# Folding a layer normalisation into centred weights and a row scale, in a graph-attention and expert kernel

## The chip, the cores and the metric

The kernel runs on one core of a Trainium2 chip. The metric is device time in microseconds (us) of one execution; shown are three runs of the kernel before and one profiled execution. The engines are TensorE (PE, with its weight loads as PEld), VectorE (DVE), ScalarE (ACT), GpSimd (POOL) and SyncE (SP), which here only issues transfers.

## The reference, cut to what matters

x is 128 graphs of 128 nodes with 256 features, adj one 128x128 matrix per graph. A graph attention comes first, then eight gated experts with three matrix products each.

```python
def _layernorm(x, axis=-1, eps=1e-5):
    m = jnp.mean(x, axis=axis, keepdims=True)
    v = jnp.var(x, axis=axis, keepdims=True)
    return (x - m) / jnp.sqrt(v + eps)
...
    Wh = jnp.einsum('bnd,df->bnf', h, W)          # h = _layernorm(x)
    s1 = Wh @ a1
    s2 = Wh @ a2
    e = s1[:, :, None] + s2[:, None, :]
    e = jnp.where(e > 0, e, ALPHA * e)
    e = e + jnp.log(adj + EPS)
    alpha_w = jax.nn.softmax(e, axis=-1)
    h_prime = jnp.einsum('bij,bjf->bif', alpha_w, Wh)
...
    x = x + _L0_gnn_ref(_layernorm(x, axis=-1), adj, L0_gnn_W, L0_gnn_a)
    x = x + _L0_ffn_ref(_layernorm(x, axis=-1), ...)
```

The change is in the first `_layernorm` and its product with `W` alone.

## The kernel before

The program has two blocks, one behind the other. The first is the attention (graph block), the second the experts (expert block). The engines meet at the border between them.

The graph block takes the graphs in 32 groups of four (`GB`), g = 0 to 31. Each engine has its own function `step(g, layer)` and runs it for every g in a row (`over_groups`), so the order of the work on an engine is the order in which `step` is written, and semaphores tie the engines together. A step works at several groups at once, by their age. Of the step that is numbered g:

- PE: transposes the attention weights of group g-2 (`ps_pT`, L741), projects group g (`ps_wide` <- `gw`, `xnT`, L730), makes the output of g-2 (`ps_th` <- `wh`, `pT`, L759, two halves of two graphs), spreads the column term s2 of g (`ps_s`, L769), transposes the normalised rows of g+1 (`ps_th` <- `ident`, `xn`, L778).
- ACT: copies `pT` (L511), takes the exponentials `e_sb` of g-1 (L518), copies the projection to `wh` (L524), normalises the rows of g+1 into `xn` (four instructions, one per graph, L501), adds s1 to give `s_sb` (L532), copies the transposed rows to `xnT` (L542), and copies the means for the second normalisation (L546).
- DVE: statistics of the rows of g+2 (`bn_stats`, L571, one per graph, and `bn_aggr`, L585), the leaky ReLU `l_sb` (L609) and the row maximum `neg_m` (L614) of g-1, a running sum `acc` for g-4 (L635, tile `resb`), `x1` of g-2 (L664, tiles `h` and `w_bc`), the weighted attention `p_sb` (L679) and its row sums (L686) of g-1, and statistics of `x1` of g-2 (L579, L590).
- POOL: from the statistics of g+2 it makes 1/sqrt(v + eps) (`rstd1`) and -mean times that (`nb1`), L400 to L407; the same for `x1` of g-3, and the other half of `acc` (L449, L453).
- SP: loads `x_sb` of g+2 (two buffers; L327), stores `x1` of g-3, loads `res` (a second copy of x, for the addition) and `adj_sb`.

On the side the steps 6 to 21 (layer 1, two per expert) prepare the first-layer weights: POOL sums pieces, in the odd step ACT rounds them (`wq_hi`, L553) and POOL then subtracts (`wq_lo`, L471). The steps 22 to 29 (layer 2) do so for the second layer (L557, L476).

Three orderings matter. The copy to `wh` of g waits for the output products of g-2 in the same step, since they read the same of the two `wh` buffers. The transposes of g+1 write the PSUM tile `ps_th` that the output products wrote, so they wait until DVE has made `x1`. SP issues the load of `x_sb` of g+2 when ACT has made `xn` of g, since it goes into the same buffer.

Ahead of step 0 PE transposes `gw` (the weights) and makes the two columns W a1 and W a2, which become columns 256 and 257 of `gw`; a projection is so 258 columns wide.

Of the kernel before, what the change touches and what calls it, by code (L numbers as in the profile page):

```python
# [38 lines left out]
def adj_ffn(nc, x, adj, gnn_w, gnn_a, wr, br, w1, b1, g1, be1, m1, v1, w2, b2, g2, be2, m2, v2, wo, bo, out):  # L39
# [17 lines left out]
    with ExitStack() as ctx:  # L57
# [127 lines left out]
        with ExitStack() as sa:  # L185
# [19 lines left out]
            minus_one = sba("minus_one", [P, GB])  # L205
            neg_mean1 = sba("neg_mean1", [P, GB])
            nb1 = [sba(f"nb1_{i}", [P, GB]) for i in range(2)]
            rstd1 = [sba(f"rstd1_{i}", [P, GB]) for i in range(2)]
            xn = sba("xn", [P, GB, D])
# [45 lines left out]
            nb1_done = sem("nb1_done", sa)  # L255
            xn_done = sem("xn_done", sa)
# [42 lines left out]
            def over_groups(eng, step):  # L299

                for i in range(-2, 2 * K0):
# [81 lines left out]
            def _(pool):  # L383
# [4 lines left out]
                nc.gpsimd.memset(minus_one[:, :], -1.0)  # L388
# [39 lines left out]
                def step(g, layer):  # L428
                    nxt = ago(g, -2)
                    if exists(nxt):  # L430
                        rstd_1(nxt)
# [14 lines left out]
                    if exists(t) and not is_step(t, G - 2) and not is_step(t, G - 1):  # L446
# [7 lines left out]
                                                ALU.add).then_inc(acc_high_done, 1)  # L454
                    if layer == 1 and g[1] == 0:
# [30 lines left out]
            def _(act):  # L486
# [8 lines left out]
                def normalise(g):  # L495

                    p = g[1]
                    act.wait_ge(nb1_done, num(g) + 1)
                    wait(act, xnT_ready, num(g))
                    for b4 in range(GB):  # L500
                        last = nc.scalar.activation(xn[:, b4, :], x_sb[p][:, b4, :], ACT.Identity,  # L501
                                                    bias=nb1[p][:, b4:b4 + 1], scale=rstd1[p][:, b4:b4 + 1])
                    last.then_inc(xn_done, 1)

                def step(g, layer):
# [20 lines left out]
                    if exists(nxt):  # L526
                        normalise(nxt)
# [37 lines left out]
            def _(dve):  # L565
# [26 lines left out]

                def step(g, layer):
                    p = g[1]
                    a = ago(g, 1)
                    r = a[1]
                    nxt = ago(g, -2)

                    def stats_part(b4):

                        if exists(nxt):
                            stats_1(nxt, b4)

                    if exists(a):

                        stats_part(0)
# [5 lines left out]
                        stats_part(1)  # L612
# [3 lines left out]
                        stats_part(2)  # L616
                        stats_part(3)
                    else:
                        for b4 in range(GB):
                            stats_part(b4)  # L620
# [5 lines left out]
                    b = ago(g, 2)  # L626
                    q = b[1]
                    t = ago(g, 3)
                    h = ago(g, 4)
                    if exists(h) and not is_step(h, G - 2) and not is_step(h, G - 1):  # L630
                        dve.wait_ge(rstd2_done, num(h) + 1)
                        dve.wait_ge(acc_low_done, num(h) + 1)
                        dve.wait_ge(mean2_done, num(h) + 1)
                        for b4 in range(HB):
                            last = nc.vector.scalar_tensor_tensor(out=acc[:, b4, :], in0=x1[h[1]][:, b4, :],  # L635
                                                                  scalar=rstd_all[:, num(h), b4:b4 + 1],
                                                                  in1=acc[:, b4, :], op0=ALU.mult, op1=ALU.add)
                        last.then_inc(acc_low_done, 1)

                    if exists(nxt):  # L640
                        dve.wait_ge(bnst1, num(nxt) + 1)
                    elif exists(b):
                        dve.wait_ge(rowsum_done, num(b) + 1)
                        if exists(t):
                            dve.wait_ge(bnst2, num(t) + 1)
                    elif exists(t):
                        dve.wait_ge(bnst2, num(t) + 1)
                    if exists(b):
                        nc.vector.reciprocal(rinv[:, :], rowsum[:, :]).then_inc(rinv_done, 1)
                    if exists(nxt):  # L650
                        aggregate_1(nxt)
                    if exists(t):
                        aggregate_2(t)
                    if exists(b):
# [5 lines left out]
                        wait(dve, x1s_high_done, num(b) - 1)  # L660
                        for b4 in range(GB):
# [8 lines left out]
                    with_stats = exists(b) and not is_step(b, G - 1)  # L670
                    if exists(a):


                        dve.wait_ge(e_done, num(a) + 1)
                        if with_stats:
                            stats_2(b, 0)
# [5 lines left out]
                        if with_stats:  # L682
                            stats_2(b, 1)
                        dve.wait_ge(p_done, num(a) + 1)
                        wait(dve, rinv_done, num(a))
                        nc.vector.tensor_reduce(rowsum[:, :], p_sb[:, :, :], AX_X, ALU.add).then_inc(rowsum_done, 1)  # L686
                    if with_stats:
                        for b4 in range(2 if exists(a) else 0, GB):
# [20 lines left out]
            def _(pe):  # L709
                pe.wait_ge(setup_done, 1)  # L710
                pe.wait_ge(proj_loaded, 2 * 16)

# [21 lines left out]
                def step(g, layer):  # L734
# [37 lines left out]
                    if exists(nxt):  # L772
                        pe.wait_ge(xn_done, num(nxt) + 1)
# [508 lines left out]
```

## Time and profile before

| | |
|---|---|
| runs | 2540.9, 2535.84, 2536.35 us, median 2536.35 |
| profiled execution | 2537.31 us; span of its instructions 2535.5 us |
| PE busy | 2412.7 us, 95% of the span |
| DVE, ACT, POOL busy | 1717.1 (68%), 1638.9 (65%), 459.4 us (18%) |
| HBM | 46 GB/s over the span |

The span is the time from the first to the last instruction of the program. Busy times overlap between engines, so the shares say which engine is full and not which one waits. The graph block is the first 390 us, some 15% of the span.

### The profile page before, as it was taken

Reading aid. Unit: us, or ns where it says so; the run is one execution under the profiler, and the core shown is the slowest. Engines: PE = TensorE matmul, PEld = TensorE weight load, DVE = VectorE, ACT = ScalarE, POOL = GpSimd, SP = SyncE. Lnnn points to the kernel's source line nnn. Section 1 sums busy time; section 2 is a strip of 40 time slices with the busy share of each in tenths; the row PEclk is TensorE's granted clock in tenths of the full one; section 3 lists DMA queues with packets and bytes.
Section 4 is the critical chain, followed back from the end, with each engine's and each line's share of the span. In section 5 each row is a group of like instructions: output and inputs, shape, how many; then the busy total and the mean of one; then the engine's idle time right before and its main releaser. Section 6 shows DMA issues by size and latency. Waiting matters only on the chain.

```text
span 2535.5 us, 45093 instructions
## 1 busy us (share of the span) xinstructions
PE 2412.7 (95%) x16304; PEld 2218.3 (87%) x16304; DVE 1717.1 (68%) x2444; ACT 1638.9 (65%) x2497; POOL 459.4 (18%) x487
## 2 busy tenths in 40 slices
PE   6777776999999999999999999999999999999999
PEld 5666665999999999999999999999999999999998
DVE  4777775666666666666666666666666666666665
ACT  4666654666666666666666666666666666666665
POOL 3566553111011111111111111111100111011110
PEclk9999997999999999999999999999999999999999
DMA  3555552000000000000000000000000000000000
GB/s 125 172 186 173 179 165 67 26 20 22 25 17 17 25 25 25 25 25 25 25 25 25 25 25 25 25 25 25 25 25 25 25 24 17 25 17 19 21 17 26
DMA packets 91178, 116.16 MB, mean 46 GB/s; under 512 B 4700, under 2 KB 78856, under 8 KB 91144
## 3 DMA queue, kind: packets, MB, share of 16 engines
q1 hardware_dynamic: 91144, 115.73, 13.9%
q8 instruction: 19, 0.31, 0.1%
q14 instruction: 15, 0.12, 0.0%
HBM read 82.16 MB, written 33.55 MB: 46 GB/s over the span
## 4 chain that ended last, share of the span: by engine, by line
PE 83%; DVE 1%; ACT 0%; issue 0%; ACTq 0%; DVEq 0%
PE ps_y L1182 29%; PE ps_wide L171 28%; PE ps_wide L1164 25%; PE ps_t L132 1%; DVE h_lo L1069 0%; DVE h L1076 0%; PE ps_y L1230 0%; DVE z L1062 0%; DVE x1t L124 0%; ACT h_hi L971 0%; DVE feat_sum L1102 0%; ACT v L976 0%; DVE resb L179 0%; DVE z L1052 0%; DVE h_lo L1084 0%
## 5 line engine op out<-in xcount | busy, mean ns | idle before, releaser
L976 ACT ACTIVATE v<-ps_wide,bn_cols 128x256 f32<-128x256 f32 x768 | 434.3, 566 | 399.3 <-PE ps_wide L1164 269.9
L984 ACT ACTIVATE h<-ps_wide,bn_cols 128x512 f32<-128x512 f32 x512 | 399.0, 779 | 327.5 <-PE ps_wide L171 327.5
L1182 PE MATMUL ps_y<-wo_lo,h_hi 128*128 128x256 f32 x2048 | 579.1, 283 | 0.0
L1182 PE MATMUL ps_y<-wo_hi,h_hi 128*128 128x256 f32 x2048 | 577.4, 282 | 1.6 <-DVE h_lo L1084 1.6
L1182 PE MATMUL ps_y<-wo_hi,h_lo 128*128 128x256 f32 x2048 | 578.6, 283 | 0.0
L1164 PE MATMUL ps_wide<-xq_hi,wq_hi 128*128 128x256 f32 x1792 | 506.2, 282 | 14.9 <-PEq L185 9.2
L1164 PE MATMUL ps_wide<-xq_lo,wq_hi 128*128 128x256 f32 x1792 | 509.7, 284 | 0.0
L1164 PE MATMUL ps_wide<-xq_hi,wq_lo 128*128 128x256 f32 x1792 | 507.1, 283 | 0.0
L1084 DVE TENSOR_TENSOR h_lo<-h,h_hi 128x1024 fp32r<-128x1024 f32 x256 | 318.2, 1243 | 238.9 <-ACT h_hi L990 238.9
L1062 DVE SCALAR_TENSOR_TENSOR z<-ps_wide,bn_cols,v 128x512 f32<-128x512 f32 x256 | 192.2, 751 | 318.0 <-PE ps_wide L1164 318.0
L171 PE MATMUL ps_wide<-h_hi,w_hi 128*128 128x512 f32 x1024 | 404.3, 395 | 2.1 <-DVE h_lo L1069 2.1
L171 PE MATMUL ps_wide<-h_lo,w_hi 128*128 128x512 f32 x1024 | 405.6, 396 | 0.0
L171 PE MATMUL ps_wide<-h_hi,w_lo 128*128 128x512 f32 x1024 | 405.5, 396 | 0.0
L1069 DVE SCALAR_TENSOR_TENSOR h_lo<-z,h_hi 128x1024 fp32r<-128x1024 f32 x256 | 316.3, 1236 | 120.7 <-ACT h_hi L971 120.7
L1182 PEld LDWEIGHTS ps_y<-wo_hi,h_hi 128*128 128x128 f32 x2048 | 386.7, 189 | 1.9 <-DVE h_lo L1084 1.8
L1182 PEld LDWEIGHTS ps_y<-wo_hi,h_lo 128*128 128x128 f32 x2048 | 387.5, 189 | 0.0
L1182 PEld LDWEIGHTS ps_y<-wo_lo,h_hi 128*128 128x128 f32 x2048 | 386.6, 189 | 0.0
L1164 PEld LDWEIGHTS ps_wide<-xq_hi,wq_hi 128*128 128x128 f32 x1792 | 341.1, 190 | 27.6 <-issue 10.0
L954 POOL TENSOR_TENSOR resb<-resb,bias_out 128x1024 f32<-128x1024 f32 x32 | 85.2, 2663 | 1535.3 <-DMA resb<-x_scratch 1535.3
L1164 PEld LDWEIGHTS ps_wide<-xq_hi,wq_lo 128*128 128x128 f32 x1792 | 338.4, 189 | 10.0
L1164 PEld LDWEIGHTS ps_wide<-xq_lo,wq_hi 128*128 128x128 f32 x1792 | 339.9, 190 | 0.0
L1076 DVE TENSOR_TENSOR h<-h,w_bc 128x1024 f32<-128x1024 f32 x256 | 312.9, 1222 | 7.5 <-ACT w_bc L1018 4.6
(131 smaller groups left out, 3118.9 us busy)
## 6 DMA issues: line engine op xcount, KB each, us to landing
x_sb<-in_x SPq DMA_DIRECT2D x32, 512.0 KB, 3.9
res<-in_x SPq DMA_DIRECT2D x32, 512.0 KB, 5.8
x1t<-x_scratch SPq DMA_DIRECT2D x32, 512.0 KB, 3.3
resb<-x_scratch SPq DMA_DIRECT2D x32, 512.0 KB, 3.3
out<-resb SPq DMA_DIRECT2D x32, 512.0 KB, 3.0
adj_sb<-in_adj SPq DMA_DIRECT2D x32, 256.0 KB, 6.0
x_scratch<-h SPq DMA_DIRECT2D x16, 512.0 KB, 4.7
x_scratch<-w_bc SPq DMA_DIRECT2D x16, 512.0 KB, 4.5
```

What stands on the lines that cost most here:

```text
L132: last = nc.tensor.transpose(ps_x[:, c, b4 * N:(b4 + 1) * N], x1t[:, b4, c * P:(c + 1) * P], ident[:, :])
L171: mm = nc.tensor.matmul(acc_ps, w[:, i, c, cols], s[:, c, :], start=start and n == 0, stop=stop and n == len(terms) - 1)
L954: nc.gpsimd.tensor_tensor(resb[:, :, :], resb[:, :, :], bias_out[:, None, :].to_broadcast([P, GB, D]), ALU.add).then_inc(resb_done, 1)
L976: nc.scalar.activation(v[:, slot, :], ps_l1[:, 0, 0:H], ACT.Identity, bias=bn_cols[:, 1, cols], scale=bn_cols[:, 0, cols]).then_inc(done, 1)
L984: nc.scalar.activation(h2[:, m, :], ps_l2[:, m, :], ACT.Relu, bias=bn_cols[:, 3, cols], scale=bn_cols[:, 2, cols]).then_inc(r2_done, 1)
L1062: nc.vector.scalar_tensor_tensor(out=z[:, 0, :], in0=ps_l1[:, 1, :], scalar=bn_cols[:, 0, C * e:C * e + 1], in1=v[:, 0:2, :].rearrange("p ...
L1069: nc.vector.scalar_tensor_tensor(out=h1_lo[:, :, :], in0=z[:, :, :], scalar=0.0, in1=h1_hi[:, :, :].bitcast(F32), op0=ALU.max, op1=ALU.sub ...
L1076: nc.vector.tensor_tensor(h2w[:, :, :].rearrange("p c (b n) -> p (c b) n", n=N), h2[:, :, :].rearrange("p c (b n) -> p (c b) n", n=N), w_b ...
L1084: nc.vector.tensor_tensor(h2_lo[p][:, :, :], h2w[:, :, :], h2_hi[p][:, :, :].bitcast(F32), ALU.subtract).then_inc(lo2_done, 1)
L1164: mm = nc.tensor.matmul(out_ps, w[:, e, q, :], x[:, q, :], start=start and n == 0, stop=stop and n == len(terms) - 1, skip_group_check=True)
L1182: mm = nc.tensor.matmul(ps_y[:, b4, :], h[:, c, cols], w[:, e, c, :], start=(e == 0 and k == 0 and b4 % per_bank == 0), stop=(e == E - 1 a ...
```

## The change

The normalised rows (x - mean) r, with r = 1/sqrt(v + eps) of the row, times W, are the same as r times x (W - column means of W). The change uses that:

- Setup: POOL fills `mean_w` with 1/256. Two PE products of 256 columns (L704 of the changed kernel) put the column means of `gw` in all rows of a PSUM tile, and DVE subtracts them from `gw` (L582, 128x512) before `gw` is transposed. `neg_mean1`, `nb1`, `minus_one` and `xn` go.
- ACT no longer makes `xn` (four instructions of 128x256 with a pointer for bias and one for scale). PE transposes `x_sb` itself. The copy to `wh`, one instruction of 128x1032, becomes four of 128x258, each with `rstd1` as a pointer for scale, and also waits for `rstd1`.
- DVE takes the statistics of g+1 in place of g+2, behind `x1` of g-2 and around `p_sb`, and no longer at the start of its step; `bn_aggr` stands behind the row sums. The two `acc` additions stand on both sides of `neg_m`.
- POOL makes `rstd1` of g+1 at the end of its step, behind the work for the second normalisation: two instructions in place of four.
- SP issues the load of g+2 when PE has transposed `x_sb` of g and DVE has taken its statistics.
- The loop begins at -1, no longer at -2.

```diff
@@ load
-                    wait(sp, xn_done, num(g) - 1)
+                    wait(sp, xnT_ready, num(g) - 1)
+                    wait(sp, bnst1, num(g) - 1)
@@ rstd_1 on POOL
-                    wait(pool, nb1_done, num(g))
-                    nc.gpsimd.tensor_tensor(ve1[:, :], mv1[p][:, :, 1], eps_cols[:, :], ALU.add)
-                    nc.gpsimd.tensor_tensor(neg_mean1[:, :], mv1[p][:, :, 0], minus_one[:, :],
-                                            ALU.mult).then_inc(ve1_done, 1)
+                    wait(pool, rstd1_done, num(g))
+                    nc.gpsimd.tensor_tensor(ve1[:, :], mv1[p][:, :, 1], eps_cols[:, :],
+                                            ALU.add).then_inc(ve1_done, 1)
                     pool.wait_ge(ve1_done, num(g) + 1)
+                    wait(pool, wh_copied, num(g) - 1)
                     nc.gpsimd.tensor_tensor(rstd1[p][:, :], ve1[:, :], minus_half[:, 0:GB],
                                             ALU.pow).then_inc(rstd1_done, 1)
-                    pool.wait_ge(rstd1_done, num(g) + 1)
-                    nc.gpsimd.tensor_tensor(nb1[p][:, :], neg_mean1[:, :], rstd1[p][:, :],
-                                            ALU.mult).then_inc(nb1_done, 1)
@@ ACT
                     if exists(g):
                         act.wait_ge(wh_ready, num(g) + 1)
+                        act.wait_ge(rstd1_done, num(g) + 1)
                         wait(act, h_ready, num(g) - 1)
-                        nc.scalar.activation(wh[p][:, :, :], ps_wide[:, :, 0:D + 2], ACT.Copy).then_inc(wh_copied, 1)
+                        for b4 in range(GB):
+                            last = nc.scalar.activation(wh[p][:, b4, :], ps_wide[:, b4, 0:D + 2], ACT.Copy,
+                                                        scale=rstd1[p][:, b4:b4 + 1])
+                        last.then_inc(wh_copied, 1)
                     nxt = ago(g, -1)
-                    if exists(nxt):
-                        normalise(nxt)
@@ DVE, setup
+                dve.wait_ge(col_mean_ready, 1)
+                nc.vector.tensor_tensor(gw[:, :, 0:D], gw[:, :, 0:D], ps_wide[:, 0:1, 0:D].to_broadcast([P, C, D]),
+                                        ALU.subtract).then_inc(gw_centred, 1)
@@ PE
+                for c in range(C):
+                    last = nc.tensor.matmul(ps_wide[:, 0, 0:D], mean_w[:, :], gw[:, c, 0:D], start=(c == 0),
+                                            stop=(c == C - 1))
+                last.then_inc(col_mean_ready, 1)
+                pe.wait_ge(gw_centred, 1)
...
-                        pe.wait_ge(xn_done, num(nxt) + 1)
+                        pe.wait_ge(x_loaded[nxt[1]], 16 * (nxt[0] + 1))
...
                                 last = nc.tensor.transpose(ps_xT[:, c, b4 * N:(b4 + 1) * N],
-                                                           xn[:, b4, c * P:(c + 1) * P], ident[:, :])
+                                                           x_sb[nxt[1]][:, b4, c * P:(c + 1) * P], ident[:, :])
```

On ACT a whole step of the graph block, as the program lists it, is this before (tile, source, shape, number):

```order
L511 ACTIVATE pT<-ps_pT 128x512
L518 ACTIVATE e_sb<-l_sb,neg_m 128x128 x4
L524 ACTIVATE wh<-ps_wide 128x1032
L501 ACTIVATE xn<-x_sb,nb_0,rstd_0 128x256 x4
L532 ACTIVATE s_sb<-ps_s,wh 128x128 x4
L542 ACTIVATE xnT<-ps_th 128x1024
L546 ACTIVATE mean_all<-mv_0 128x4
```

and this in the changed kernel, at the same place:

```order
L497 ACTIVATE pT<-ps_pT 128x512
L504 ACTIVATE e_sb<-l_sb,neg_m 128x128 x4
L512 ACTIVATE wh<-ps_wide,rstd_0 128x258 x4
L520 ACTIVATE s_sb<-ps_s,wh 128x128 x4
L530 ACTIVATE xnT<-ps_th 128x1024
L534 ACTIVATE mean_all<-mv_1 128x4
```

The row of `xn` is gone, and the copy to `wh` has four parts and reads `rstd`.

On DVE a step ran in this order (from the start of the step, step 5 of the graph block, to `p_sb`):

```order
L571 BN_STATS st<-x_sb 128x6
L609 SCALAR_TENSOR_TENSOR l_sb<-s_sb 128x512
L571 BN_STATS st<-x_sb 128x6
L614 TENSOR_REDUCE neg_m<-l_sb 128x4
L571 BN_STATS st<-x_sb 128x6 x2
L635 SCALAR_TENSOR_TENSOR resb<-w_bc,rstd_all,resb 128x256 x2
L649 RECIPROCAL rinv<-rowsum 128x4
L585 BN_AGGR mv_1<-st 128x2 x4
L590 BN_AGGR mv_0<-st 128x2 x4
L664 SCALAR_TENSOR_TENSOR w_bc<-ps_th,rinv,res 128x256 x4
L579 BN_STATS st<-w_bc 128x6
L679 SCALAR_TENSOR_TENSOR p_sb<-adj_sb,e_sb 128x512
```

and in the changed kernel the same step runs so:

```order
L617 SCALAR_TENSOR_TENSOR l_sb<-s_sb 128x512
L621 RECIPROCAL rinv<-rowsum 128x4
L578 BN_AGGR mv_0<-st 128x2 x4
L604 SCALAR_TENSOR_TENSOR resb<-w_bc,rstd_all,resb 128x256
L627 TENSOR_REDUCE neg_m<-l_sb 128x4
L604 SCALAR_TENSOR_TENSOR resb<-w_bc,rstd_all,resb 128x256
L647 SCALAR_TENSOR_TENSOR w_bc<-ps_th,rinv,res 128x256 x4
L559 BN_STATS st<-x_sb 128x6 x2
L661 SCALAR_TENSOR_TENSOR p_sb<-adj_sb,e_sb 128x512
L559 BN_STATS st<-x_sb 128x6 x2
L567 BN_STATS st<-w_bc 128x6
L674 TENSOR_REDUCE rowsum<-p_sb 128x4
```

The statistics of x have moved from ahead of `l_sb` to behind `x1` (tile `w_bc`), and nothing of `x_sb` stands between the step's start and `x1` any more. PE's order is the same in both, but for the two products at the start; only what the transposes read and wait for differs.

## Rows read from the trace of the kernel before

**Rows 1.** Page: busy share in 40 equal slices, and granted PE clock, in tenths.

```profile
PE   6777776999999999999999999999999999999999
PEclk9999997999999999999999999999999999999999
```

**Rows 2.** Timeline, 204 to 218 us, all engines: start us, length us.

```profile
204.34 0.39 SPq L327 DMA_DIRECT2D x_sb<-in_x  x1
...
206.43 3.75 PE L730 MATMUL ps_wide<-gw,xnT 128*128 128x258 f32 x16 [0.68 <-ACT xnT L542]
...
208.39 0.43 DVE L571 BATCH_NORM_STATS2 st<-x_sb 128x6 f32<-128x256 f32 x1 [2.17 <-DMA x_sb<-in_x]
...
210.02 1.89 PE L759 MATMUL ps_th<-wh,pT 128*128 128x256 f32 x8
...
210.36 1.28 ACT L518 ACTIVATE e_sb<-l_sb,neg_m 128x128 f32<-128x128 f32 x4 [3.41 <-DVE neg_m L614]
...
212.01 1.03 ACT L524 ACTIVATE wh<-ps_wide 128x1032 f32<-128x1032 f32 x1 [0.36 <-PE ps_th L759]
...
212.93 2.06 ACT L501 ACTIVATE xn<-x_sb,nb,rstd 128x256 f32<-128x256 f32 x4
...
213.09 1.16 PE L769 MATMUL ps_s<-ident,wh 128*128 128x128 f32 x8 [1.18 <-ACT wh L524]
...
214.90 1.11 ACT L532 ACTIVATE s_sb<-ps_s,wh 128x128 f32<-128x128 f32 x4
215.05 1.09 PE L778 MATMUL ps_th<-ident,xn 128*128 128x128 f32 x8 [0.80 <-ACT xn L501]
...
216.18 1.02 ACT L542 ACTIVATE xnT<-ps_th 128x1024 f32<-128x1024 f32 x1 [0.16 <-PE ps_th L778]
...
217.25 3.75 PE L730 MATMUL ps_wide<-gw,xnT 128*128 128x258 f32 x16 [0.68 <-ACT xnT L542]
```

**Rows 3.** Groups, 100 to 400 us, shapes apart: busy us, mean ns.

```profile
L501 ACT ACTIVATE xn<-x_sb,nb,rstd 128x256 f32<-128x256 f32 x96 | 49.5, 588 | 0.0
...
L571 DVE BATCH_NORM_STATS2 st<-x_sb 128x6 f32<-128x256 f32 x88 | 34.8, 416 | 54.9 <-DMA x_sb<-in_x 54.9
...
L532 ACT ACTIVATE s_sb<-ps_s,wh 128x128 f32<-128x128 f32 x100 | 27.9, 358 | 1.2 <-PE ps_s L769 1.2
...
L524 ACT ACTIVATE wh<-ps_wide 128x1032 f32<-128x1032 f32 x25 | 25.6, 1024 | 16.4 <-PE ps_th L759 16.4
...
L511 ACT ACTIVATE pT<-ps_pT 128x512 f32<-128x512 f32 x26 | 15.3, 589 | 2.6 <-PE ps_pT L741 2.6
```

**Rows 4.** Timeline of PE, projections and one transpose of 30 steps.

```profile
38.97 3.79 PE L730 MATMUL ps_wide<-gw,xnT 128*128 128x258 f32 x16 [0.26 <-ACT xnT L542]
...
69.29 1.52 PE L778 MATMUL ps_th<-ident,xn 128*128 128x128 f32 x8 [0.80 <-ACT xn L501]
71.93 4.37 PE L730 MATMUL ps_wide<-gw,xnT 128*128 128x258 f32 x16 [0.26 <-ACT xnT L542]
...
361.52 3.75 PE L730 MATMUL ps_wide<-gw,xnT 128*128 128x258 f32 x16 [0.68 <-ACT xnT L542]
```

**Rows 5.** Busy time and granted clock (after POOL's entry) by stretch.

```profile
70.00:71.00 1.00, 1.00 (x6) 1.00 (x5) 0.69 (x3) 0.40 (x2) 0.92 (x2) 0.50 0.81 72
...
200.00:250.00 50.00, 37.58 (x200) 30.94 (x199) 40.29 (x129) 34.19 (x80) 31.73 (x49) 0.97 0.51 163
```

**Rows 6.** Timeline, 196 us: POOL and DVE side by side.

```profile
196.34 2.08 POOL L471 TENSOR_TENSOR wq_lo<-w_stage,wq_hi 128x896 f32 x1 [1.11 <-ACT wq_hi L553]
...
196.74 2.23 DVE L609 SCALAR_TENSOR_TENSOR l_sb<-s_sb 128x512 f32<-128x512 f32 x1
```

**Rows 7.** Timeline of the start, PE and DVE.

```profile
15.95 6.71 PE L730 MATMUL ps_wide<-gw,xnT 128*128 128x258 f32 x16 [1.40 <-ACT xnT L542]
...
27.95 3.75 PE L730 MATMUL ps_wide<-gw,xnT 128*128 128x258 f32 x16 [1.11 <-ACT xnT L542]
...
29.70 0.43 DVE L571 BATCH_NORM_STATS2 st<-x_sb 128x6 f32<-128x256 f32 x1 [12.80 <-DMA x_sb<-in_x]
```

More of the change, by code:

```diff
@@ L204, in adj_ffn @@
             ve1 = sba("ve1", [P, GB])
-            minus_one = sba("minus_one", [P, GB])
-            neg_mean1 = sba("neg_mean1", [P, GB])
-            nb1 = [sba(f"nb1_{i}", [P, GB]) for i in range(2)]
+            mean_w = sba("mean_w", [P, P])
             rstd1 = [sba(f"rstd1_{i}", [P, GB]) for i in range(2)]
-            xn = sba("xn", [P, GB, D])
             xnT = sba("xnT", [P, C, T])
@@ L299, in over_groups @@
             def over_groups(eng, step):
-                for i in range(-2, 2 * K0):
+                for i in range(-1, 2 * K0):
                     step((i // 2, i % 2), 0)
@@ L493, in _ @@
                                      ACT.Copy).then_inc(va_copied, 1)
[L495 to L503, printed above, removed]
                 def step(g, layer):
@@ L591, in aggregate_2, with add_part @@
                     last.then_inc(stats2_done, 1)
+                dve.wait_ge(col_mean_ready, 1)
+                nc.vector.tensor_tensor(gw[:, :, 0:D], gw[:, :, 0:D], ps_wide[:, 0:1, 0:D].to_broadcast([P, C, D]),
+                                        ALU.subtract).then_inc(gw_centred, 1)
                 def step(g, layer):
-                    p = g[1]
                     a = ago(g, 1)
+                    b = ago(g, 2)
+                    t = ago(g, 3)
+                    h = ago(g, 4)
                     r = a[1]
[L597 to L602, printed above, removed]
+                    q = b[1]
+                    nxt = ago(g, -1)
+                    with_acc = exists(h) and not is_step(h, G - 2) and not is_step(h, G - 1)
+                    with_stats = exists(b) and not is_step(b, G - 1)
+                    def add_part(b4):
+                        if not with_acc:
+                            return
+                        if b4 == 0:
+                            dve.wait_ge(rstd2_done, num(h) + 1)
+                            dve.wait_ge(acc_low_done, num(h) + 1)
+                            dve.wait_ge(mean2_done, num(h) + 1)
+                        part = nc.vector.scalar_tensor_tensor(out=acc[:, b4, :], in0=x1[h[1]][:, b4, :],
+                                                              scalar=rstd_all[:, num(h), b4:b4 + 1],
+                                                              in1=acc[:, b4, :], op0=ALU.mult, op1=ALU.add)
+                        if b4 == HB - 1:
+                            part.then_inc(acc_low_done, 1)
+                    if exists(b):
+                        dve.wait_ge(rowsum_done, num(b) + 1)
+                    if exists(t):
+                        dve.wait_ge(bnst2, num(t) + 1)
                     if exists(a):
-                        stats_part(0)
                         dve.wait_ge(s_done, num(a) + 1)
@@ L615, in step @@
                                                 negate=True).then_inc(neg_m_done, 1)
[L616 to L620, printed above, removed]
+                    add_part(1)
                     if is_step(g, G - 1):
@@ L625, in step @@
                         tile_normalise(dve, 0, range(HB, GB))
[L626 to L653, printed above, removed]
                     if exists(b):
@@ L669, in step @@
                         last.then_inc(x1_done, 1)
-                    with_stats = exists(b) and not is_step(b, G - 1)
+                    if exists(nxt):
+                        wait(dve, rstd1_done, num(nxt) - 1)
+                        stats_1(nxt, 0)
+                        stats_1(nxt, 1)
                     if exists(a):
                         dve.wait_ge(e_done, num(a) + 1)
-                        if with_stats:
-                            stats_2(b, 0)
                         dve.wait_ge(adj_loaded[r], 16 * (a[0] + 1))
@@ L686, in step @@
                         nc.vector.tensor_reduce(rowsum[:, :], p_sb[:, :, :], AX_X, ALU.add).then_inc(rowsum_done, 1)
+                    if exists(nxt):
+                        aggregate_1(nxt)
                     if with_stats:
-                        for b4 in range(2 if exists(a) else 0, GB):
+                        for b4 in range(1, GB):
                             stats_2(b, b4)
```

33 lines of the change are left out of this document (24 added, 9 removed).

## The prediction

> **What bounds the kernel now.** I read the page first. PE is busy 9 tenths or more from the seventh slice on, with the full clock, and 5 to 7 tenths before [rows 1]. The reader is to see two programs: an expert block in which PE is full, which this change doesn't touch, and a graph block of some 370 us in which PE is not full and something goes round in a ring. All that can be won or lost lies there (and at its two ends).
>
> Then the timeline of one step. Follow PE from one projection to the next, 206.43 to 217.25, which is 10.82 us [rows 2]. The projection and the output products end at 210.02 + 1.89 = 211.91. ACT's copy to `wh` starts 0.10 later. It takes 1.03, and the normalisation of the next rows ends at 214.99. PE waits 0.80 for that and transposes (1.09), ACT copies the result (1.02, start 216.18), and the next projection starts at 217.25 [rows 2]. Nothing in this ring has slack: it is PE, ACT, PE, ACT, PE. The column term (`ps_s`, 1.16) and `s_sb` (1.11) lie beside the normalisation and cost nothing [rows 2].
>
> A second ring is nearly as long. ACT ends `xn`, SP issues a load at 204.34, DVE waits 2.17 us for it and starts at 208.39; the leaky ReLU and the maximum stand behind this, and ACT waits 3.41 for the maximum before it takes the exponentials (210.36 to 211.64), which stand ahead of the copy to `wh` [rows 2]. Here that left 0.36 us to spare. Over the block DVE waited 54.9 us for x [rows 3].
>
> Thirty projections stand between 38.97 and 361.52: 322.55 us, or 11.12 for each of 29 steps [rows 4]. 29 undisturbed steps would be 29 x 10.82 = 313.8. The other 8.8 us are two things. First the clock: it fell to half seven times in this stretch, each time as the transposes ran or were about to. In the fall at 69.8 the transposes took 1.52 in place of 1.09 and the projection 4.37 in place of 3.75 [rows 2, 4, 5], so 1.05 us; at 1.0 each, 7.0. Ahead of such a fall PE had waited 1.18 us, spread the column term, and waited 0.80 [rows 2]. Second, eight odd steps with `wq_lo` on POOL: `l_sb` on DVE took 2.23 us beside POOL's 2.08 [rows 6], the exponentials came late, and that leaves 1.8 us for all.
>
> **The change, part by part.** *The normalisation goes, the copy to `wh` grows.* The price of one 128x258 copy with one pointer has no row of its own. Its nearest is `s_sb`: from PSUM, one pointer, 128 columns, 358 ns [rows 3]. The slope of ACT per column is (1024 - 589) / (1032 - 512) = 0.84 ns, from two plain copies out of PSUM [rows 3]; 130 more columns are 109 ns, so 467. Four `s_sb` take 1.11 [rows 2], so the next starts 251 ns after the one before, and 107 of 358 overlap. Four copies: 467 + 3 x 360 = 1.55 us. From below: without a price for the pointer, 376 and 3 x 269, 1.18 us. From above: like `xn`, with two pointers and 256 columns, 2.06 us [rows 2]. I take 1.55, since `s_sb` has the same source and one pointer, and keep 1.18 and 2.06 for the range.
>
> The Trainium skill, page "ScalarE: Activation LUTs", section "What ACT_TABLE_LOAD costs", gives an instruction with immediates 186 ns + 0.833 per column, 93 more for each pointer, and an overlap of about 93; by that estimate the four would take 1.70, and the sum below would be some 4 us less.
>
> *The new ring.* Output products end, 0.10, copy to `wh` 1.55, 0.05, column term 1.16, 0.03, `s_sb` 1.12 less 0.11 by which the next instruction on ACT starts before its end, copy to `xnT` 1.02, 0.05, projection and output products 5.48 (206.43 to 211.91) [rows 2]. The transposes stand right behind the column term on PE and take 1.09, so they lie beside `s_sb`. Sum: 0.10 + 1.55 + 0.05 + 1.16 + 0.03 + 1.01 + 1.02 + 0.05 + 5.48 = 10.45 us, 0.37 less than now. So of the 2.06 us of ACT work that goes only 0.37 come out, because the column term and `s_sb` lose their cover: they were beside the normalisation and are now in the ring. 29 x 0.37 = 10.7 us.
>
> *The load of x.* The transposes of g now free the buffer a step ahead of its next reader, and DVE reads it a step later. From the issue (as now, 204.34) to the first statistics, right behind `x1` of the next step but one, there are more than 15 us, against 4.05 now [rows 2]. The wait goes. The projection no longer waits for the chain behind it.
>
> *DVE's step.* What it does per step is the same: 40.29 us busy of 50, 9.0 per step of 11.12 [rows 5]. In a step of 10.45 there is room. Late next would be the exponentials. `s_sb` is ready 3.9 us behind the start of the copy to `wh`; DVE is free about 5 behind it (x1, four statistics, `p_sb`, row sums, two aggregations, three more statistics); `l_sb`, the reciprocal, an aggregation, half the `acc` and the maximum take 2.3, so the exponentials end at 8.6, against 10.45. If `wq_lo` (2.08 [rows 6]) blocks one of them, 10.3 to 10.6: just covered or 0.2 late. I count the 1.8 us as won, and in eight steps 0.2 as lost (1.6).
>
> *POOL and SP.* `rstd1` is made at 4 to 6 us of a step and read at 10.45: covered. Queued behind it are only the weight pieces, which have two steps. SP's loads wait for things of the step before; behind them stand a store and two loads that have a step to spare.
>
> *The clock.* Between the output products and the transposes PE now waits 1.18 + 0.80; it will wait 1.55 + 0.15 once, and column term and transposes run on without a gap. Less idle time in sum (1.70 for 1.98) but in one piece. That could end the falls or make them more frequent. No row decides it; I take two for seven, 5.0 us won, and keep both ends (7.0 won, 8.4 lost).
>
> *The start.* Four more PE records at the half clock (6.71 / 16 = 0.42 each [rows 7]) and one DVE instruction of 512 columns, near the 0.59 of a copy of that size [rows 3], some 2.4 with the waits. The first normalisation (2.06) goes. So +0.5. The first step (15.95 to 27.95) has the same ring: -0.37. The second, 27.95 to 38.97, took 11.02 because DVE sat until 29.70 for x [rows 4, 7]; without output products its ring is 10.45 - 5.48 - 0.10 + 3.75 + 0.05 = 8.67: -2.35.
>
> *The end.* The last steps have no normalisation before either, and a longer copy to `wh`: +0.5.
>
> **Sum.** 10.7 + 1.8 - 1.6 + 5.0 - 0.5 + 0.37 + 2.35 - 0.5 = 17.6 us off the profiled execution's 2537.31, so 2519.7. That execution is 1.0 above the median of the runs (2536.35), so a run is 2519 us.
>
> **The rivals.**
> 1. *The clock falls in every second step.* 14 or 15 falls at 1.1 in place of seven at 1.0: 17.6 - 5.0 - 8.4 = 4.2 won, 2532. For it: one wait of 1.70 is longer than either of now. Against: PE's work behind it has no gap.
> 2. *Slower: the copy to `wh` costs like `xn`.* At 2.06 the ring is 10.96, and 29 x 0.14 = 4.1 are lost; from 1.92 on the ring is no shorter than now. PE's wait is then 2.2 us in one piece, and the falls of rival 1 come with it: -4.1 + 1.8 - 1.6 - 8.4 + 1.7 = -10.6, 2547; without more falls 2539. Against: `s_sb` shows what one pointer costs.
> 3. *No change: DVE ends last.* If POOL's instructions block DVE's in all steps and not only in eight, the exponentials come at 10.8 or later, the ring is as now, and only the start and a part of the clock are won: 2533 to 2538. The Trainium skill, page "GPSIMD Engine Reference", section "Specifications", says that GpSimd shares its SBUF interface with VectorE instructions that have two SBUF inputs, as `l_sb` and the `acc` additions have. The trace agrees in the one pair [rows 6]. Against: POOL's other instructions are mostly 1 us or less.
> 4. *Better: the copy is near 1.2 us.* Ring 10.1, but then the exponentials (10.2) end last: 2513.
>
> **How the numbers follow.** Chances: the forecast with few or no falls 0.55; rival 1 0.16; rival 2 0.12; rival 3 0.10; rival 4 0.07. This kernel's measurement tells 0.2%, 5 us, from no change. Faster: the forecast, rival 4 and half of rival 1, 0.70; within 5 us: the other half of rival 1 and most of rival 3, 0.17; slower 0.13. The forecast's own range is 2514 to 2526. The range for 8 in 10 goes from rival 4's side to rival 1 and the near end of rival 3: 2512 to 2537.
>
> **What would show it.** Right: DVE waits for x no more; four copies to `wh` take 1.5 to 1.6 in sum; steps of 10.4 to 10.5 from projection to projection; `xnT` starts as `s_sb` ends; the second step is near 8.7. Wrong: copies over 1.8; the exponentials ending right ahead of the copy to `wh` in steps without `wq_lo`; more stretches at a clock of 0.50 than now; or a wait of PE for `x_sb`.

## The result, and the profile after

| | before | after |
|---|---|---|
| median of the runs | 2536.19 us (4 runs) | 2515.58 us (4 runs, 2515.3 to 2516.79) |
| profiled execution, span | 2537.31, 2535.5 us | 2515.62, 2513.8 us |
| ratio after / before | | 0.9915, 95% interval 0.9898 to 0.9933 |
| third projection starts | 38.97 us | 36.08 us |
| last projection, 29 steps on | 361.52 us | 340.77 us |
| first product of the expert block | 390.19 us | 370.19 us |

The change is 20.6 us faster, where 17 were forecast and the range was 2512 to 2537. Nearly all of it, 20.0 us, lies ahead of the expert block. The other 1.7 of the 21.7 by which the spans differ lie in the expert block, which the change doesn't touch. In the profiled executions of the ten kernels of this document that block took between 2143.6 and 2146.6 us, so a difference of this size says nothing of an edit in the graph block.

Every time here is a median; one execution of `stats_first` (3429.95 us, mean granted clock 0.65) and one of the kernel before that was timed beside it (8351.13 us) are far outside the rest and left out.

The page of the changed kernel, busy share and granted clock of PE in 40 slices, is to be laid beside [rows 1]:

```profile
PE   6777769999999999999999999999999999999999
PEclk9999988999999999999999999999999999999999
```

PE gets full from the seventh slice on, one earlier than before (there it was the eighth, and not the seventh as the prediction reads it). Its timeline for one step (start us, length us; in brackets the idle time before and what ended it), to be laid beside [rows 2]:

```profile
204.23 3.76 PE L726 MATMUL ps_wide<-gw,xnT 128*128 128x258 f32 x16 [0.84 <-ACT xnT L530]
...
205.31 2.08 POOL L467 TENSOR_TENSOR wq_lo<-w_stage,wq_hi 128x896 f32 x1 [0.59 <-ACT wq_hi L541]
205.39 2.29 DVE L604 SCALAR_TENSOR_TENSOR resb<-h,rstd_all,resb 128x256 f32<-128x256 f32 x1
...
207.60 0.67 DVE L627 TENSOR_REDUCE neg_m<-l_sb 128x4 f32<-128x512 f32 x1
207.83 1.89 PE L755 MATMUL ps_th<-wh,pT 128*128 128x256 f32 x8
...
208.31 1.28 ACT L504 ACTIVATE e_sb<-l_sb,neg_m 128x128 f32<-128x128 f32 x4 [2.71 <-DVE neg_m L627]
...
209.76 1.58 ACT L512 ACTIVATE wh<-ps_wide,rstd 128x258 f32<-128x258 f32 x4 [0.17 <-PE ps_th L755]
...
211.39 1.16 PE L765 MATMUL ps_s<-ident,wh 128*128 128x128 f32 x8 [1.67 <-ACT wh L512]
...
212.38 1.04 PE L774 MATMUL ps_th<-ident,x_sb 128*128 128x128 f32 x8
...
212.58 1.14 ACT L520 ACTIVATE s_sb<-ps_s,wh 128x128 f32<-128x128 f32 x4 [1.25 <-PE ps_s L765]
...
213.60 1.04 ACT L530 ACTIVATE xnT<-ps_th 128x1024 f32<-128x1024 f32 x1
...
214.69 3.76 PE L726 MATMUL ps_wide<-gw,xnT 128*128 128x258 f32 x16 [0.84 <-ACT xnT L530]
```

Read it as the prediction's ring: output products end at 209.72, the four copies to `wh` take 1.58, the column term follows 0.05 behind them, the transposes run on behind it without a wait, and `xnT` starts as `s_sb` ends. From projection to projection it is 10.46 us. The next step, without `wq_lo`, takes 10.54, since its copy to `wh` starts 0.12 behind the output products (end 220.18) in place of 0.04:

```profile
220.30 1.58 ACT L512 ACTIVATE wh<-ps_wide,rstd 128x258 f32<-128x258 f32 x4 [1.91 <-PE ps_th L755]
```

The projections of the first steps and the last (timeline of PE), beside [rows 4, 7]:

```profile
16.57 5.81 PE L726 MATMUL ps_wide<-gw,xnT 128*128 128x258 f32 x16 [1.40 <-ACT xnT L530]
...
27.35 3.76 PE L726 MATMUL ps_wide<-gw,xnT 128*128 128x258 f32 x16 [1.27 <-ACT xnT L530]
...
36.08 3.76 PE L726 MATMUL ps_wide<-gw,xnT 128*128 128x258 f32 x16 [0.84 <-ACT xnT L530]
...
340.77 3.76 PE L726 MATMUL ps_wide<-gw,xnT 128*128 128x258 f32 x16 [0.84 <-ACT xnT L530]
```

The groups between 100 and 370 us (busy us, mean ns of one, idle before them and what ended it), beside [rows 3]. DVE waits for x no more (0.0 against 54.9):

```profile
L512 ACT ACTIVATE wh<-ps_wide,rstd 128x258 f32<-128x258 f32 x96 | 37.8, 477 | 27.2 <-PE ps_th L755 27.2
...
L559 DVE BATCH_NORM_STATS2 st<-x_sb 128x6 f32<-128x256 f32 x92 | 34.2, 412 | 0.0
```

And the windows of 100 to 360 us (busy of PE, PEld, DVE, ACT, POOL, then the granted clock), first before:

```profile
100.00:360.00 260.00, 198.39 (x1026) 163.54 (x1027) 200.25 (x626) 171.79 (x393) 162.23 (x232) 0.96 0.55 178
```

and after:

```profile
100.00:360.00 260.00, 195.28 (x1071) 164.18 (x1070) 226.54 (x670) 144.67 (x385) 163.36 (x192) 0.99 0.58 186
```

Between the first step and 355.3 us no stretch at half clock is left; before there were eight, seven of them in the 29 steps. The clock of 0.99 over the window is the stretch from 355.3 on, where PE waits at the block's end. So 29 steps gave 322.55 - 304.69 = 17.9 us, in two parts. The undisturbed ring gave 313.8 (29 x 10.82) less 304.5 (15 x 10.54 and 14 x 10.46), which is 9.3. What was lost beside it, 8.8 us before, is 0.2 now: 8.6 more. Those 8.6 are the falls of the clock and the late odd steps together.

### The profile page after: what moved, and what is told of

It is laid out like the page before. It is cut to its first block, busy times and chain, and to the rows that moved or that the text cites. A ratio compares the mean times of both kernels' runs of the same rounds, so it can differ in the third digit from the quotient of the medians.

```text
span 2513.8 us, 45142 instructions
## 1 busy us (share of the span) xinstructions
PE 2397.0 (95%) x16308; PEld 2209.6 (88%) x16308; DVE 1729.6 (69%) x2445; ACT 1596.0 (63%) x2465; POOL 453.7 (18%) x423
## 4 chain that ended last, share of the span: by engine, by line
PE 84%; DVE 1%; ACT 0%; issue 0%; ACTq 0%
PE ps_y L1178 29%; PE ps_wide L171 29%; PE ps_wide L1160 26%; PE ps_t L132 1%; DVE h_lo L1065 0%; DVE h L1072 0%; PE ps_y L1226 0%; DVE z L1058 0%; ACT v L972 0%; DVE h_lo L1080 0%; ACT h_hi L986 0%; ACT h_hi L967 0%; ACT w_bc L1014 0%; ACT h L980 0%; DVE z L1048 0%
```

## The experiments

Three questions: whether the clock's falls cost what the prediction took, and what ends them; what the copy's price does to the ring; and what the late statistics bring. Then a version that the trace suggested. Each kernel was timed against the kernel before (medians beside them 2536.8 to 2538.5 us); the steps quoted are from one projection to the next.

### Two pointers in the copy to `wh`

The changed kernel, with the four copies given a second pointer, to a column of zeros. The numbers are the same. This brings about rival 2's price.

```diff
-                            last = nc.scalar.activation(wh[p][:, b4, :], ps_wide[:, b4, 0:D + 2], ACT.Copy,
-                                                        scale=rstd1[p][:, b4:b4 + 1])
+                            last = nc.scalar.activation(wh[p][:, b4, :], ps_wide[:, b4, 0:D + 2], ACT.Identity,
+                                                        bias=zero_col[:, :], scale=rstd1[p][:, b4:b4 + 1])
```

> The changed kernel, with a second pointer (a bias column of zeros) on each of the four copies to wh. Computes the same. Theory (the step is a ring through the copies, and the clock falls where PE waits long in one piece): the four copies take about 2.05 in place of 1.58 us, the ring becomes 10.50 + 0.47 = 10.97, 14 us in 30 steps, and PE's wait of 2.2 us brings stretches at a clock of 0.50 back, 5 or more, 5 to 13 us: 2535 to 2543. Rival (the falls went for another reason, such as the transposes of raw rows): no falls, 2529 to 2530. Second rival (the copies have slack): 2516.

Measured: 2537.93 us (10 runs), 1.0002 of before, interval 0.9992 to 1.0011: the whole win is gone. The four copies take 1.94, not the 2.05 expected. The edit also turns `Copy` into `Identity`; `s_sb` is an `Identity` with one pointer, and its price gave that of a `Copy` with one pointer within 10 ns, so the second pointer is the likely cause, but no run separates the two. The timeline shows the dearer copy and PE's longer wait:

```profile
78.56 1.94 ACT L514 ACTIVATE wh<-ps_wide,zero_col,rstd 128x258 f32<-128x258 f32 x4 [3.26 <-PE ps_th L757]
...
80.55 1.16 PE L767 MATMUL ps_s<-ident,wh 128*128 128x128 f32 x8 [2.11 <-ACT wh L514]
```

Undisturbed steps are 10.81 and 10.89, 0.35 longer than after, which is 10 us in 29. The rest is the clock. It falls again in the middle of the block, at 69.8, 114.2, 158.6, 202.9 and further on, and in the first of these the transposes took 1.85 in place of 1.04. PE's wait was 2.03 or 2.11 in nearly every step, and nine of the 29 had a fall: such a wait doesn't bring one each time. The window of the first:

```profile
69.80:73.20 3.40, 3.14 (x15) 2.74 (x13) 3.18 (x16) 2.69 (x7) 1.46 (x4) 0.50 0.07 14
```

### The same, with PE kept busy in the wait

Six products of the identity with itself, into a tile that is free then, between the output products and the column term. They change no number of the kernel's.

```diff
+                    if exists(b):
+                        for b4 in range(6):
+                            nc.tensor.matmul(ps_pT[:, b4 % GB, :], ident[:, :], ident[:, :], start=True, stop=True)
                     if exists(g):
                         pe.wait_ge(wh_copied, num(g) + 1)
```

> The kernel two_pointers, and PE does six more products of ident with itself (12 records of 128 columns, about 1.5 us) into the free ps_pT in its wait between the output products and the column term; nothing reads them. Theory: ring as in two_pointers, 10.97, but no stretch at a clock of 0.50 inside the graph block: 2529 to 2531, so the difference of the two kernels is the price of the falls. Rival (the ring alone makes the time, the clock is not bound to PE's waits): the same time as two_pointers.

Measured: 2528.49 us (6 runs), 0.9969 (0.9957 to 0.9982). The steps are still 10.81 and 10.89, and after one fall in the start (33 to 37 us) the clock doesn't fall until 378 us, as the window of the steps shows:

```profile
100.00:350.00 250.00, 213.97 (x1294) 188.63 (x1294) 203.78 (x624) 145.31 (x361) 155.15 (x182) 1.00 0.58 185
```

So of the 22.4 us that the second pointer costs, 9.4 are the clock's falls and 12.9 the longer ring, with what it adds at the start and the end. With a wait of PE of 2.0 to 2.1 us there were falls, with 1.7 to 1.8 in the changed kernel there were none.

### The kernel before, with PE kept busy in its second wait

Three such products between the column term and the transposes, in the kernel before.

```diff
                         last.then_inc(s2b_ready, 1)
+                    if exists(b):
+                        for b4 in range(3):
+                            nc.tensor.matmul(ps_pT[:, b4 % GB, :], ident[:, :], ident[:, :], start=True, stop=True)
                     if exists(nxt):
                         pe.wait_ge(xn_done, num(nxt) + 1)
```

> The kernel before, and PE does three more products of ident with itself (6 records of 128 columns, about 0.75 us) into the free ps_pT in its wait of 0.80 us between the column term and the transposes; nothing reads them. Theory: the eight falls of the clock in the graph block go, the undisturbed step stays 10.82, and about 7 us are won: 2529. Rival (the falls are not bound to this wait, or the products lengthen the ring): 2536 or more, with falls.

Measured: 2529.34 us (9 runs), 0.997 (0.996 to 0.998), 7.9 us faster. The timeline of PE has its 0.80 wait filled, and from output products to transposes nothing else moved; the window behind it has the full clock:

```profile
209.85 1.16 PE L769 MATMUL ps_s<-ident,wh 128*128 128x128 f32 x8 [1.18 <-ACT wh L524]
210.84 0.83 PE L774 MATMUL ps_pT<-ident 128*128 128x128 f32 x6
211.81 1.09 PE L781 MATMUL ps_th<-ident,xn 128*128 128x128 f32 x8
```

```profile
100.00:360.00 260.00, 211.14 (x1197) 176.85 (x1198) 202.70 (x637) 174.09 (x400) 163.45 (x235) 1.00 0.56 181
```

All seven falls of the 29 steps are gone; one in the start, at 35.8, stays. The traces put less on them than the medians do: the 29 steps take 316.42 us (39.07 to 355.49) in place of 322.55, so 6.1, and the graph block is 6.0 shorter. The steps with `wq_lo` are 11.09 with the clock full, 0.27 over the 10.82 of the others. So of the 8.8 us lost beside the undisturbed ring before, 6.1 were the falls and 2.6 late steps, mostly those with `wq_lo` (the prediction had 7.0 and 1.8). All in all the falls cost 6 to 8 us.

The falls needed PE's second wait: with the 0.80 filled and the 1.18 as it was, there were none in the steps. But most steps of the kernel before had both waits and no fall. The change has one wait of 1.67 to 1.75 in their place and no gap behind it, and its trace has no fall in the steps.

### The kernel before, with the statistics of x late

Here DVE takes the statistics of x behind `x1`, as in the change, and POOL makes `rstd1` and `nb1` at its step's end; the normalisation stays on ACT.

```diff
@@ POOL: rstd_1(nxt) from the step's start to behind the acc addition
@@ DVE: ahead of l_sb, between l_sb, neg_m and acc
-                        if exists(nxt):
-                            stats_1(nxt, b4)
@@ DVE: behind x1, around p_sb
+                    if exists(nxt):
+                        stats_1(nxt, 0)
+                        stats_1(nxt, 1)
...
+                    if exists(nxt):
+                        stats_1(nxt, 2)
+                        stats_1(nxt, 3)
```

> The kernel before with only the order of DVE and POOL changed: the statistics of x of g+2 behind x1 and around p_sb, their aggregation behind the row sums, and rstd1 and nb1 at the end of POOL's step. Normalisation, transposes and copies stay. Theory: DVE waits for x no more, undisturbed step still 10.82 since that ring has no DVE in it; won are the late odd steps (1.8 us) and about 2 us at the start, falls stay: 2532 to 2533. Rival (the wait for x is what bound the step before): 2525 or less. Rival (the falls shift with the step): 2530 to 2538.

Measured: 2532.51 us (10 runs), 0.998 (0.9971 to 0.999), 4.7 us faster. The wait for x is gone and steps are 10.83 and 10.77, but the falls stay (seven in the 29 steps). So the new order of DVE's work is not what ended the falls in the changed kernel. In its timeline the exponentials end at 206.6 and the copy to `wh` starts at 208.93, so the second ring has 2.3 us to spare where it had 0.36 [rows 2]:

```profile
205.34 1.28 ACT L518 ACTIVATE e_sb<-l_sb,neg_m 128x128 f32<-128x128 f32 x4 [1.46 <-DVE neg_m L613]
...
208.93 1.03 ACT L524 ACTIVATE wh<-ps_wide 128x1032 f32<-128x1032 f32 x1 [2.31 <-PE ps_th L763]
```

Of the 4.7, the start gave 0.8 (third projection at 38.17; about 2 was expected) and the 29 steps 2.2 (358.54 - 38.17 = 320.37); 0.1 more lies between there and the expert block. The other 1.6 are not in the graph block; in the profiled execution the expert block was 1.2 shorter, within its spread. That the time fell into the range expected was in part luck.

### The changed kernel, with the statistics first

The four statistics of g+1 go back to the start of DVE's step, ahead of `l_sb`; all else as changed.

```diff
+                    if exists(nxt):
+                        wait(dve, rstd1_done, num(nxt) - 1)
+                        for b4 in range(GB):
+                            stats_1(nxt, b4)
                     if exists(a):
                         dve.wait_ge(s_done, num(a) + 1)
```

> The changed kernel, with DVE's four statistics of x of g+1 put back to the start of its step, ahead of the leaky ReLU (where they stood before, though then for g+2). Theory (what counted in DVE's step was the wait for the load, and raw rows are now there a step ahead; DVE's work per step is the same and it is free 1.3 us earlier to do it): no wait for x, leaky ReLU at the same time, 2515 to 2517. Rival (the place of the statistics itself is what keeps the exponentials early): they come 1.3 us later, which the eight steps with wq_lo can't hide, 2522 to 2527.

Measured: 2516.28 us (3 runs; 0.9913, interval 0.9892 to 0.9935), steps of 10.54 and 10.46 as in the change. The order of the statistics is worth nothing here. The exponentials start 4.07 us behind the projection, in the change 4.08: DVE reads rows that have long been there, and what it no longer does behind `x1` it does here, so `l_sb` behind the four statistics starts 0.32 after the projection, in the change 0.20:

```profile
202.73 1.41 DVE L559 BATCH_NORM_STATS2 st<-x_sb 128x6 f32<-128x256 f32 x4 [0.32 <-DVE st L567]
204.05 0.67 DVE L621 SCALAR_TENSOR_TENSOR l_sb<-s_sb 128x512 f32<-128x512 f32 x1
```

The wait goes wherever the load is issued long enough ahead of its first reader, here a whole step. In the kernel before, moving the reader back in its step was enough.

### Transposes ahead of the column term

The change leaves the column term and `s_sb` in the ring, though the next projection needs neither. Here PE transposes x of g+1 ahead of the column term of g, and ACT copies `xnT` ahead of `s_sb`.

```diff
@@ ACT: xnT ahead of s_sb
+                    if exists(nxt):
+                        act.wait_ge(xnT_ready, num(nxt) + 1)
+                        wait(act, wh_ready, num(nxt))
+                        nc.scalar.activation(xnT[:, :, :], ps_xT, ACT.Copy).then_inc(xnT_copied, 1)
                     if exists(g):
                         act.wait_ge(s2b_ready, num(g) + 1)
@@ PE: the column term behind the transposes
                         last.then_inc(xnT_ready, 1)
+                    if exists(g):
+                        pe.wait_ge(wh_copied, num(g) + 1)
...
+                        last.then_inc(s2b_ready, 1)
```

> The changed kernel, with PE's transposes of x of g+1 ahead of the column term of g, and ACT's copy to xnT ahead of s_sb. Both are free to go there since raw rows wait for nothing of ACT's. Theory (column term and s_sb stand in the ring since the change): the transposes run in PE's wait for wh, and of 2.2 us (column term 1.16, s_sb 1.04) about 1.1 come out; undisturbed steps 9.3 to 9.5. The exponentials then end last in the eight odd steps with wq_lo, 10.2 to 10.4, and steps with w_lo are 9.5 to 10: sum 18 to 26 us less than the changed kernel, 2490 to 2498. Rival (DVE's nine us of work per step and the collisions with POOL bind at once): 2505 to 2513. No falls of the clock by the first theory, since PE waits less.

Measured: 2488.78 us (4 runs), 0.9804 (0.9787 to 0.9822), a little better than expected. But the parts were not as expected: layer 0 steps take 8.56 (9.3 to 9.5 expected), those of layer 2 9.39 and 9.5, in layer 1 they alternate between 8.9 to 9.4 and 11.2 to 11.5 (10.2 to 10.4 expected), and there are falls of the clock where none was expected. In an odd step PE now waits for x1:

```profile
208.87 2.36 POOL L467 TENSOR_TENSOR wq_lo<-w_stage,wq_hi 128x896 f32 x1
...
209.57 1.95 DVE L604 SCALAR_TENSOR_TENSOR resb<-h,rstd_all,resb 128x256 f32<-128x256 f32 x1
...
213.64 1.44 PE L766 MATMUL ps_th<-ident,x_sb 128*128 128x128 f32 x8 [2.12 <-DVE h L647]
...
214.93 2.08 PE L774 MATMUL ps_s<-ident,wh 128*128 128x128 f32 x8
```

DVE's addition is held up by `wq_lo`, the maximum and `x1` behind it come late, PE waits 2.12 us, and then the clock falls to half: the column term takes 2.08 in place of 1.16. Eight such falls stand in layer 1, 20.5 us apart, as this one:

```profile
112.40:115.80 3.40, 3.40 (x15) 3.21 (x14) 3.40 (x12) 2.54 (x7) 0.76 (x3) 0.50 0.18 23
```

### The row maximum ahead of both additions

The same, with the maximum moved ahead of the first half of `acc` too.

```diff
-                    add_part(0)
                     if exists(a):
                         dve.wait_ge(l_done, num(a) + 1)
                         nc.vector.tensor_reduce(neg_m[:, :], l_sb[:, :, :], AX_X, ALU.max,
                                                 negate=True).then_inc(neg_m_done, 1)
+                    add_part(0)
                     add_part(1)
```

> The kernel transpose_first, with DVE's row maximum ahead of both additions to acc, so that an addition held up by POOL's wq_lo no longer holds up the maximum. Theory: the exponentials of the eight odd steps come up to 2 us earlier, those steps fall from 10.3 towards 9.5 unless DVE's own step binds them, so 3 to 7 us less than transpose_first, 2484 to 2494. Rival (the additions only move the delay to x1, which the transposes wait for): the same as transpose_first or more.

Measured: 2480.29 us (4 runs), 0.9771 (0.9753 to 0.9788), 56 to 58 us under the kernel before and 35 under the change, and better than the 2484 to 2494 expected, which counted no falls of the clock. No fall of the clock up to 320 us; layer 1 steps are 8.77 and 10.31. In the odd step PE's wait for x1 is shorter, and it waits once more, for `p_sb`:

```profile
219.36 0.65 DVE L626 TENSOR_REDUCE neg_m<-l_sb 128x4 f32<-128x512 f32 x1
...
219.93 1.79 DVE L604 SCALAR_TENSOR_TENSOR resb<-h,rstd_all,resb 128x256 f32<-128x256 f32 x2
...
222.86 1.35 PE L766 MATMUL ps_th<-ident,x_sb 128*128 128x128 f32 x8 [1.50 <-DVE h L647]
...
224.07 1.63 DVE L661 SCALAR_TENSOR_TENSOR p_sb<-adj_sb,e_sb 128x512 f32<-128x512 f32 x1
...
225.76 0.66 PE L737 MATMUL ps_pT<-ident,p_sb 128*128 128x128 f32 x4 [0.66 <-DVE p_sb L661]
```

### Transposes first, with PE kept busy in the wait for x1

Was that the maximum, or the clock? Here the maximum stays behind the first addition, and PE has four products of the identity ahead of the transposes.

```diff
+                    if exists(b):
+                        for b4 in range(4):
+                            nc.tensor.matmul(ps_pT[:, b4 % GB, :], ident[:, :], ident[:, :], start=True, stop=True)
                     if exists(nxt):
                         pe.wait_ge(x_loaded[nxt[1]], 16 * (nxt[0] + 1))
```

> transpose_first with four products of the identity with itself, into the free tile ps_pT, between PE's output products and its transposes, in each step with output products: the numbers of the kernel don't change. It asks how much of what transpose_max_first won over transpose_first (8.5 us) was the clock. The trace of transpose_first has eight falls of TensorE's clock in layer 1, one in every second step, and the odd steps there take 11.3 to 11.5 us. Theory A, the clock alone: with PE busy in the wait for x1 the falls go, the odd steps come to about 10.3, and the time is 2480, as with the maximum first. Theory B, the late maximum alone: the falls go but the row maximum still stands behind the addition that GpSimd's wq_lo holds up, the exponentials stay late and the odd steps stay over 11: 2486 to 2488. In between, about 1 us for a fall: eight falls are 8 us of the 8.5, and I expect 2481 to 2484, nearer to A.

Measured: 2479.19 us (4 runs), 0.9773 (0.9757 to 0.979). That is the time of `transpose_max_first` within a thousandth, with the exponentials as late as in `transpose_first` (6.02 us behind the projection in both):

```profile
202.20 0.67 DVE L627 TENSOR_REDUCE neg_m<-l_sb 128x4 f32<-128x512 f32 x1
...
202.90 1.28 ACT L504 ACTIVATE e_sb<-l_sb,neg_m 128x128 f32<-128x128 f32 x4 [3.97 <-DVE neg_m L627]
...
204.40 1.35 PE L769 MATMUL ps_th<-ident,x_sb 128*128 128x128 f32 x8 [1.24 <-DVE h L647]
```

Steps are 8.91 and 10.30, 19.21 for two against 19.08 with the maximum first. So the 9.6 us between `transpose_first` and this kernel are the clock, and those to `transpose_max_first` (8.5) nearly all; the late maximum by itself costs some 0.13 in two steps, about 1 us in all. My guess of 2481 to 2484 gave it too much. It mattered because it lengthened PE's wait.

## Why the prediction held, step by step

- **The ring.** Forecast 10.45 us; measured 10.46 and 10.54. The four copies were put at 1.55 and took 1.58, `xnT` starts as `s_sb` ends, and the transposes lie beside `s_sb`, as said. Forecast for 29 steps 10.7, measured 9.3. The copy's price came from `s_sb` and a slope, and 467 ns was put for one where 477 was measured. The 1.4 us that the ring gave less are 0.05 a step, of which the copies are 0.03 and `xnT` 0.02. That the column term and `s_sb` stand in the new ring is read off the timeline, and confirmed by the kernels that take them out. The Trainium skill, page "ScalarE: Activation LUTs", section "What ACT_TABLE_LOAD costs", led to an estimate of 1.70 for the four; the trace has 1.58, so the row of the nearest instruction was the better guide.
- **The load of x.** DVE's wait of 54.9 us went to nothing, and the odd steps' late exponentials with it: 1.8 counted as won. The two kernels that bear on this term alone put it at 2.2 (`before_late_stats`) and 2.6 (what `before_pe_busy` leaves).
- **Late exponentials beside `wq_lo`.** Forecast 0.2 us in eight steps, 1.6. It did not happen. In a step without `wq_lo` they ended 8.6 behind the copy to `wh`, as said; with it the place was right (DVE's addition took 2.29 beside `wq_lo`, the maximum came at 207.60), and the exponentials end at 209.59 with 0.17 to spare before the copy to `wh`: "just covered" was the case, at the near end of the bounds. The Trainium skill, page "GPSIMD Engine Reference", section "Specifications", says that GpSimd shares its SBUF interfaces with VectorE and contends with VectorE instructions of two SBUF inputs, and the trace agrees: such an addition took 2.29 beside `wq_lo`, and the next one, beside a POOL instruction of 128x4, 0.47.
- **The clock.** This term was mis-sized: forecast two falls for seven and 5.0 us, measured none, so 6.1 to 7.0. The two of seven were a guess between two ends, as the prediction says. That filling a wait ends the falls, and what they cost, is shown by the kernels with PE kept busy, in which the ring was the same (7.9 and 9.4 us).
- **The start.** Ahead of the first projection +0.62 (forecast 0.5), the second step 8.73 (8.67). The first step gave 1.22, not 0.37: its projection took 5.81, not 6.71 [rows 7]. Before, all of it ran at about 0.42 for a product; now the last third ran at the later, faster pace. The prediction calls this start the half clock from the lengths alone: the rows of the granted clock read 1.00 there in both kernels. Why the pace rose earlier stays open, so this 0.85 was luck.
- **The end.** +0.75, forecast +0.5.
- **The sum.** 9.3 + 1.8 - 0.2 + 7.0 for the 29 steps, 2.9 at the start, -0.75 at the end: 20.0 by the trace, 17.6 by the forecast. The misses were +1.6 (exponentials), +2.0 (clock), +0.8 (first step), less 1.4 (ring), 0.2 (the rest in odd steps) and 0.4 at the start and the end. In part they cancel: 4.4 one way, 2.0 the other.
- **The rivals.** Rival 2 was right as a mechanism: with the copies at 1.94 (break-even was put at 1.92) the kernel is as slow as before. The ring is no shorter than before, and the falls, eleven up to 360 us where before there were eight, took what the load and the start would have given. Rival 1 did not come: PE's single wait of 1.67 to 1.75 us brought no fall, while one of 2.0 to 2.1 did in the kernel with two pointers. Rival 3 did not come: without `wq_lo` the maximum started 1.71 behind the projection, with it 3.37. (POOL has others of 1.0 to 1.3 us, more than the "mostly 1 us or less" of the prediction, but the exponentials had 1.9 to spare.) Rival 4 had no chance at 1.58.

The reading that the gain is small because the column term and `s_sb` lose their cover is borne out by the version that takes them out of the ring: it is 27 us faster than the change, though it takes out more than them, since the transposes then also lie beside the copy to `wh`.

## What to carry to other kernels

When an edit takes work off a ring, redraw the ring: what was hidden beside the removed work may now be its tail, and here moving that tail behind the transposes was worth more than the edit. Sum also how long PE waits in a piece ahead of each burst of work: an edit of a few tenths in a wait decided whether the clock fell, and that was worth about as much as the shorter ring; a few idle products show cheaply how much of a difference it is. A price from the nearest row, with the same engine, source and number of pointers, came within 2%.

## What the runs showed of the hardware

- The granted clock (1.2 GHz at 0.50, 2.4 GHz at 1.00) fell time and again in the middle of the graph block. Waits of 1.18 and 0.80 around a short burst, or a single one of 2.0 to 2.1, stood ahead of such falls; a single one of 1.7 to 1.8 did not. Most steps with the longer waits had no fall either (seven falls in 29 steps before, nine with two pointers), and what else decides it is open. Filling a wait with products that do nothing won 7.9, 9.4 and 9.6 us in three kernels.
- With a second pointer, to a constant zero (and `Identity` for `Copy`), four ACT copies of 128x258 from PSUM took 1.94 in place of 1.58 us.
- A DVE addition with two SBUF inputs took 1.95 to 2.29 us beside a long POOL instruction of 2.08 to 2.37, in place of 0.45 to 0.47. Through the maximum and `x1` behind it, that lengthened a wait of PE, and through the wait it cost clock.
